# The delta stage's group loop: a value product ahead of the third gate, transposes, copies and activations in another order

## The reference, cut to what matters

```
qkv = silu(causal_conv1d(x @ W_qkvz, conv_weight))         # 4 taps
attn = -(k_beta @ k.T) * decay_mask, strictly lower         # chunks of 64 tokens
attn = row-by-row correction of attn, + I                   # inverse of a triangular matrix
v = attn @ v_beta;  k_cum = attn @ (k_beta * exp(g))
for each chunk:                                             # carries state
    v_prime = v_c - k_cum_c @ state
    out     = (q_c @ state) * exp(g) + intra @ v_prime
    state   = state * exp(g_last) + (k_c * decay).T @ v_prime
out = rmsnorm(out * silu(z), norm_weight) @ W_out
```

## Time and profile before

| | |
|---|---|
| median of three runs | 1714.47 us (1711.51 to 1717.37) |
| the profiled execution's own time | 1714.89 us |
| its span, first to last instruction | 1713.2 us |
| mean granted PE clock over the span | 0.915 of full speed |
| PE / DVE / ACT / POOL busy, share of the span | 83% / 67% / 50% / 46% |
| loop over the groups, about | 550 to 1570 us |
| from one `l1p` on PE to the next | 61.9 to 66.4 us |

### The profile page before, as it was taken

One profiled execution on the slowest core, in us unless ns is written; L12 is line 12 of the kernel. 1 busy time (PEld: TensorE's weight loads), 2 busy tenths in 40 slices (PEclk: granted clock), 3 DMA queues, 4 the chain that ended last, 5 costly groups with the idle time before them and its releaser, 6 DMA issues. The chain is left out here.

```text
span 1713.2 us, 38604 instructions
## 1 busy us (share of the span) xinstructions
PE 1428.9 (83%) x14345; PEld 1025.2 (60%) x14345; DVE 1139.4 (67%) x2334; ACT 856.3 (50%) x2403; POOL 780.6 (46%) x1118
## 2 busy tenths in 40 slices
PE   5888993199555889999999999999999999986665
PEld 2443442166422667767767767767777777775465
DVE  6886127823566778788778777778788878643623
ACT  3334861043043575665665665665665666532122
POOL 5000000277114266456556466556566656553343
PEclk9998996599776999999999999999999999988688
DMA  8100005085813464554555555654555545241783
GB/s 280 66 2 2 2 1 154 7 234 178 254 49 88 107 146 124 147 149 134 139 146 139 128 152 134 139 147 142 133 147 149 137 143 151 76 117 56 223 259 128
DMA packets 249434, 218.72 MB, mean 128 GB/s; under 512 B 88770, under 2 KB 224962, under 8 KB 247200
## 3 DMA queue, kind: packets, MB, share of 16 engines
q1 hardware_dynamic: 234992, 192.41, 41.4%
q0 software_dynamic: 5712, 15.60, 2.8%
q10 hardware_dynamic: 8544, 8.26, 1.5%
HBM read 133.85 MB, written 82.25 MB: 126 GB/s over the span
## 5 line engine op out<-in xcount | busy, mean ns | idle before, releaser
L1544 PE MATMUL d_big<-all_xn_t,all_w 128*128 128x512 f32 x512 | 264.2, 649 | 17.3 <-DVE d_conv L1805 11.4
L1805 DVE SCALAR_TENSOR_TENSOR d_conv<-d_big,all_cw,d_conv 128x1023 f32<-128x1023 f32 (+2 forms) x192 | 245.4, 1278 | 46.4 <-ACT d_conv L2039 43.8
L2277 POOL TENSOR_TENSOR d_y<-d_y,all_xn 128x256 f32<-128x256 f32 x128 | 95.8, 748 | 183.9 <-DVE d_y L1952 153.0
L1544 PEld LDWEIGHTS d_big<-all_xn_t,all_w 128*128 128x128 f32 x512 | 98.2, 207 | 107.8 <-issue 96.7
L2141 ACT COPY d_ys<-d_big 128x128 f32<-128x128 f32 x256 | 60.9, 266 | 198.5 <-PE d_big L1695 139.5
L1733 PE MATMUL d_big<-all_wo,d_yt 128*128 128x256 f32 x512 | 126.5, 393 | 13.6 <-DVE d_yt L1877 13.6
L1666 PE MATMUL d_big<-all_w,all_xn_t 128*128 128x256 f32 x512 | 124.2, 386 | 0.0
L1851 DVE SCALAR_TENSOR_TENSOR d_AI<-d_big,d_b_col,d_decay 128x256 f32<-128x256 f32 x256 | 105.7, 474 | 23.0 <-PE d_big L1557 20.7
L1733 PEld LDWEIGHTS d_big<-all_wo,d_yt 128*128 128x128 f32 x512 | 97.4, 198 | 26.4 <-issue 14.1
L1666 PEld LDWEIGHTS d_big<-all_w,all_xn_t 128*128 128x128 f32 x512 | 93.6, 190 | 18.3 <-issue 7.2
L347 DVE TENSOR_REDUCE a_neg_max<-a_big 128x1 f32<-128x128 f32 (+7 forms) x128 | 90.5, 751 | 13.1 <-PE a_big L276 12.8
(11 more groups left out here) (437 smaller groups left out, 3503.5 us busy)
## 6 DMA issues: line engine op xcount, KB each, us to landing
turned_kq_scratch<-d_turned SPq DMA_DIRECT2D x32, 512.0 KB, 3.9
d_kq_tok<-turned_kq_scratch SPq DMA_DIRECT2D x128, 128.0 KB, 3.1
turned_v_scratch<-d_vs SPq DMA_DIRECT2D x16, 1024.0 KB, 4.1
d_vs<-turned_v_scratch SPq DMA_DIRECT2D x64, 256.0 KB, 5.6
grouped_y_scratch<-d_yx SPq DMA_DIRECT2D x32, 512.0 KB, 3.9
d_yx<-grouped_y_scratch SPq DMA_DIRECT2D x128, 128.0 KB, 3.1
all_w<-in_L_attn_W_qkvz SPq DMA_DIRECT2D x16, 768.0 KB
l_hold<-in_L_ffn_gate_up_proj SPq DMA_DIRECT2D x48, 192.0 KB, 3.4
```

The source lines that it names most:

```text
L1544: mm = pe.matmul(big[0][:, c, :], w_sb[par][:, k, n * DK:(n + 1) * DK], xn_t[:, k, c * 512:(c + 1) * 512], start=(k == 0), stop=(k == KD - 1))
L1805: dve.scalar_tensor_tensor(conv[:, sh:T], src[:, 0:T - sh], cw[:, bass.ds(g, 1), COLUMN_OF[j], 3 - sh], conv[:, sh:T], ALU.mult, ALU.add). ...
L2277: pool.tensor_tensor(part, part, zs[:, t, :], ALU.mult).then_inc(s["yg_s"], 1)
```

## The change

In `PE_ORDER`, `prev iv 7` moves from behind `gates 3` to just ahead of `gates 2`, and `l2y` moves ahead of `products 2`. In `DVE_ORDER`, `gather 7` goes between tap 1 and tap 2 of projection 1, the first two transposes `l0x 0`, `l0x 1` go ahead of its tap 3, DVE's `l1p` goes right behind that tap, followed by the third transpose, and only then `kq_turn 1`; `l2p` goes ahead of `products 0`. In `ACT_ORDER`, `l1p` goes ahead of `silu 1`, `gates 3` directly behind `silu 1`, and all four `ksq` and `decay` behind it. To allow this `l0x` is split into three steps of one transpose each. The computation, the tiles and the semaphore counts are the same.

```diff
-    l0y 2, gates 2, l0y 3, l0y 4, l0y 5, l0y 6, l0y 7, gates 3; prev iv 7; this l1p 0, l1p 1, l1p 2, l1p 3; next proj 2
+    l0y 2; prev iv 7; this gates 2, l0y 3, l0y 4, l0y 5, l0y 6, l0y 7, gates 3, l1p 0, l1p 1, l1p 2, l1p 3; next proj 2
...
-            def l0x(g, par):
-
-                for n, q in enumerate((0, 2, 1)):
-                    own = slice(QB * q, QB * q + QB)
-                    half_of = slice(QB * (q % 2), QB * (q % 2) + QB)
-                    dve.wait_ge(s["y0_s"], g * 4 + n + 1)
-                    dve.transpose(Xc[own, :, half_of], Y[own, :, own]).then_inc(s["x0_s"], 1)
+            def l0x(g, par, n):
+
+                q = (0, 2, 1)[n]
+                own = slice(QB * q, QB * q + QB)
+                half_of = slice(QB * (q % 2), QB * (q % 2) + QB)
+                dve.wait_ge(s["y0_s"], g * 4 + n + 1)
+                dve.transpose(Xc[own, :, half_of], Y[own, :, own]).then_inc(s["x0_s"], 1)
```

More of the change, by code:

```diff
@@ L1209 @@
     0, l0p 1, l0p 2, l0p 3, l0p 4; next proj 1 0; this l0p 5, l0p 6, l0p 7; prev qs 7; next proj 1 1; this l0y 0, l0y 1,
-    l0y 2, gates 2, l0y 3, l0y 4, l0y 5, l0y 6, l0y 7, gates 3; prev iv 7; this l1p 0, l1p 1, l1p 2, l1p 3; next proj 2
-    0, proj 2 1; this l1y 0, l1y 1, l1y 2, l1y 3; next products 0; this l2p 0, l2p 1; next products 1, products 2; this
-    l2y 0, l2y 1; next products 3; this y 0, kv 0, iv 0, ks 1; prev out_mm 0 0; this y 1, qs 1, kv 1, iv 1, ks 2, qs 2;
+    l0y 2; prev iv 7; this gates 2, l0y 3, l0y 4, l0y 5, l0y 6, l0y 7, gates 3, l1p 0, l1p 1, l1p 2, l1p 3; next proj 2
+    0, proj 2 1; this l1y 0, l1y 1, l1y 2, l1y 3; next products 0; this l2p 0, l2p 1; next products 1; this l2y 0, l2y 1;
+    next products 2, products 3; this y 0, kv 0, iv 0, ks 1; prev out_mm 0 0; this y 1, qs 1, kv 1, iv 1, ks 2, qs 2;
     prev out_mm 0 1; this y 2, kv 2, iv 2, ks 3, y 3, qs 3, kv 3, iv 3; next proj 3 0; this ks 4; next proj 3 1; this y
@@ L1218 @@
     prev state 6; this v_turn 0; prev r 7, gather 5; this v_turn 1; next tap 0 1, tap 0 2, tap 0 3; this qe; next
-    kq_turn 0; prev gather 6; this l0p; next shift, tap 1 1, tap 1 2, tap 1 3; prev gather 7; this l0x; next kq_turn 1;
-    this l1p; prev y_turn 0; next kb; this l1y; next products 0; this l2p; next products 1; this l2y; next products 2;
+    kq_turn 0; prev gather 6; this l0p; next shift, tap 1 1; prev gather 7; next tap 1 2; this l0x 0, l0x 1; next tap 1
+    3; this l1p, l0x 2; next kq_turn 1; prev y_turn 0; next kb; this l1y, l2p; next products 0, products 1; this l2y; next products 2;
     this state 0, gather 0, r 1; next products 3; this state 1, gather 1; next tap 2 1; this r 2; next tap 2 2; this
@@ L1228 @@
     prev sq2 0, o1 5, sq2 1, ys 6, sq2 2, sq2 3; this silu 3; next tap0 0; this gates 0; prev ys 7, o1 6; next silu 0;
-    this gates 1; prev sq2 4, o1 7; next tap0 1; prev sq2 5; this gates 2, l0y; next silu 1, ksq 0, ksq 1, ksq 2; this
-    l1p; next ksq 3, decay; this gates 3, l1y, l2p; prev sq2 6, sq2 7; this l2y, ys 0; next tap0 2; this ys 1, o1 1;
+    this gates 1; prev sq2 4, o1 7; next tap0 1; prev sq2 5; this gates 2, l0y, l1p; next silu 1; this gates 3; next ksq 0, ksq 1, ksq 2, ksq 3,
+    decay; this l1y, l2p; prev sq2 6, sq2 7; this l2y, ys 0; next tap0 2; this ys 1, o1 1;
     next qsq 0; this ys 2, o1 2, ys 3, o1 3; next silu 2, qsq 1; this ys 4; next tap0 3; this o1 4, ys 5
```

## The result

The changed kernel took a median of 1749.73 us (1742.34 to 1759.92, four runs), the kernel before in the same session 1714.72 (1711.51 to 1717.37, four runs). The ratio is 1.018, 95% interval 1.0125 to 1.0243: **slower by 1.8%**, where I had forecast 1710 us and a range up to 1732. The profiled execution took 1742.34 us, 32.5 more than the 1709.8 of my sum and 27.4 more than the profiled execution of before. Here and in the experiments medians are of all runs and ratios of the fast ones, which leaves three executions of one later kernel (1710 to 1717 us, at a lower clock than its others) out of the ratios.

A forecast was written before the change was run, and what follows sets the result against it. PE bounds, with a 1.90 us wait ahead of `l1p` and clock falls behind; 0.25 x 14 = 3.5 us plus 1.6 in the last group gave 1714.89 - 5.1 = 1709.8, forecast 1710 us, own range 1700 to 1718, with rivals 1689 to 1732.

The forecast's parts named there:

- my sum: Whole kernel: 5.1 us gained in all, 1714.89 - 5.1 = 1709.8 us for the profiled execution.
- The new wait: PE ahead of `l2p`: idle of about 1.2 us, released by DVE's copy `l1y`, which stands behind `kb`.
- The interval of a clean group: From the old `l1p` place to `y 0` without a clock fall: 13.85 us instead of 13.89.
- A: PE ahead of `l2p`: the new idle seldom pulls the clock down, one group in ten; 1690 us; chance 0.24.
- E: Ahead of `l1p`: ACT's copies, not DVE's list, hold the transposes, so the wait stays; 1713 us; chance 0.04.
- D: ACT in the sweep: the moved table load makes `ys 4` 0.9 us late in 15 groups; 1723 us; chance 0.04.
- the price of a fall: PE from `l2p` to `y 0`: each clock fall costs 3.4 us, against 1.7 in `proj 2`.
- the share: Groups whose clock falls behind the new wait: half again, 0.5, seven of 14.
- the first group: `kb` is held by POOL already there, so this group gains nothing.
- the two long ones of before: Clock falls of some 6.8 us over `l2p` and `l2y`, costing 3.4 us each, taken as model for new falls.
- rival C: DVE's `kb` runs into POOL's `vs`; each hit costs 4.7 us, in five groups 1733 us; chance 0.10.
- B: PE ahead of `l2p`: the new idle pulls the clock down nearly always, share 0.85; 1726 us; chance 0.16.

The follow-up runs named there:

- e1: Changed kernel with products 2 back between l2p and l2y on PE, DVE's products 0 and 1 back ahead of l2p and l2y; 1719.5 us, ratio 1.0024 to before.
- f4: Changed kernel with two products repeated right behind products 1, between l2p and l2y, as a control; 1726.0 us, ratio 1.0035 to before.
- e3: Changed kernel with two product matmuls of the next group repeated in PE's wait ahead of l2p; 1696.8 us, ratio 0.9886 to before.
- f2: e4 with products 1 ahead of l2p on PE, so l2y follows l2p directly; 1706.8 us, ratio 0.9926 to before.
- e4: Changed kernel with ksq 0 (two squares) moved ahead of l1p on ACT; 1693.7 us, ratio 0.9789 to before.
- f3: Kernel before with two products repeated in PE's wait ahead of l1p, filling about half of it; 1727.6 us, ratio 1.0039 to before.
- g3: Kernel before with PE's wait ahead of l1p wholly filled, twice the repeated product matmuls of f3; 1722.7 us, ratio 1.0033 to before.
- f1: e4 with the filling of e3 ahead of l2p added; 1704.3 us, ratio 0.9905 to before.

## Why the prediction was wrong

**Right, point by point.** PE's wait ahead of `l1p`: 0.26 (I said 0.4). The new wait, its place, releaser and size: 1.42 for 1.2. `kb` 1309.83 - 1302.94 = 6.89 behind `l1p` (6.8). `y 0` 15.48 behind `l1p` (15.5). The interval of a clean group: unchanged. From `y 0` to the next `l1p`: 1364.77 - 1318.42 = 46.35, which is within 0.05 the 48.03 of before less the 1.64 by which `l1p` is earlier. No fall over `proj 2`. So A and E are refuted, and D too: ACT's `ys 4` still has idle ahead of it, with the load in front of `silu 2`. Timeline of ACT, to set beside the earlier trace rows:

```profile
1331.35 1.28 ACT L2051 ACT_TABLE_LOAD   x1
1332.64 1.06 ACT L2051 ACTIVATE d_vt<-d_conv 128x1024 f32<-128x1024 f32 x1
...
1335.74 0.45 ACT L2141 COPY d_ys<-d_big 128x128 f32<-128x128 f32 x2 [0.45 <-ACT d_junk L2070]
```

The load takes 1.28 us and `silu 2` starts 0.01 behind it. The Trainium skill ("ScalarE: Activation LUTs", What ACT_TABLE_LOAD costs) adds a drain of 1380 ns to it; the trace shows none here, nor in front of the load: the activation ahead of it ends at 1331.33.

**The step that failed is the price of a fall**, with the share beside it: 0.5 x 3.4 us a group, 23.8 in 14. Nine groups fell, not seven; at 3.4 us each they would have cost 30.6. They cost 50.2. So 6.8 of what was missing is the share and 19.6 the price, the longer waits of two groups with it. By groups of the changed kernel, above 21.45 us each:

| | groups | us |
|---|---|---|
| wait of 1.4, then a fall of 10.2 us | 5 | 21.4, that is 4.3 each |
| `kb` held up by `vs`, wait of 3.0 to 3.2, a fall of 13.7 | 2 | 15.3 |
| PE stops 1.7 or 2.4 us in `l1y`, a fall of 13.7 | 2 | 13.5 |
| no fall | 5 | 0.4 |

That is 50.6 where I had 23.8. With the first group (5.6 worse, where I had said no gain and no loss: its wait ahead of `l2p` is 4.46 and it falls for 13.7 instead of 3.4) and the last (1.1 gained, not 1.6) it is 26.8 + 5.6 + 0.5 = 32.9, against the 32.5 by which the profiled execution missed my sum.

Three errors are in it. I took the length of a fall from the two long ones of before (6.8 us), in which products 1 and 2 still stood between `l2p` and `l2y`, although the same change moves `products 2` away: e1 and f4 show that what stands there decides between 3.4 to 6.8 and 10 to 14 us. That makes 4.3 us for a plain fall where I had 3.4. Second, my rival C, which I gave one chance in ten, did happen, not in five groups but in two and in the first one; I priced it at 4.7 and it cost 7.7, because the longer wait drew a longer fall. DVE of such a group, and POOL at that time:

```profile
905.39 1.89 DVE L1831 TENSOR_TENSOR d_kxb<-l_cols,d_b_col 128x16 f32<-128x16 f32 x1
```

```profile
905.34 1.91 POOL L2234 TENSOR_TENSOR d_vs<-d_vs,d_sv 128x1024 f32<-128x1024 f32 x1 [6.97 <-DMA d_vs<-turned_v_scratch]
```

The instruction takes 0.18 us elsewhere. In the clean group `kb` ended 0.33 us ahead of `vs`, where I had reckoned 0.75; over the other groups the distance runs from 1.7 us to none. A few tenths of a us decide whether they meet. Third, I saw that the two long falls of before came behind stops in `l1y` and priced them with the rest; in the changed kernel two groups of that kind cost 6.7 each (in before 4.5 and 6.1), 2.9 more in all. They are no part of the share of groups that the wait decides.

And rivals A and B were set up as one question, how often the clock falls. The count did not change, nine of 14 in both kernels. What changed was the length.

What stays open: why the clock falls behind one wait of 1.41 and not behind another (five of eight groups with it), and how many groups fall, and for how long, in an execution other than the profiled one.

## What to carry to other kernels

Price a wait by what stands beside it. With one product ahead of it and small matmuls, a product and small matmuls behind it, 1.4 us of idle cost 4.0 to 4.7 us more through the clock in five of eight groups, and with the falls gone (e3) the same order was faster than before. Full matmuls behind a wait made the falls shorter (e1, f4); that they help ahead of it too is my guess from f2 against e4. Two matmuls whose result nobody reads were worth their microsecond in e3, and not in the kernel before (f3, g3) nor on top of the shorter wait (f1): measure such a filling, don't assume it. When a wait moves, look at the lengths of the falls it will meet in the new place, not only at their number. And the source of a wait is worth more than its place: one pair of squares moved ahead on ACT gave 1.5 to 2.1% over the kernel before (1.3 and 1.6% by the medians of all executions), where the change without it lost 1.8%.

## What the runs showed of the hardware

PE stops in the middle of `l1y`, 96 matmuls of 32x32 that take 1.2 us when nothing stops them, for 0.4 to 3.2 us, released by nothing in the profile ("issue"). The traces hold the fetches of instructions as DMA packets on queue q8, 16 KiB each, one in some 11 us. In g3 such a fetch begins 2.4 to 2.8 us before the end of each of the nine stops in `l1y`, and 2.4 to 3.0 before the end of each of the five in the kernel before. Not every fetch beside `l1y` stops PE: in the first group of before one begins 0.1 us into it, and it still takes 1.2. DMA queues in the stretch 628 to 631, with the stop that ends at 630.62 (queue, packets, MB, share of the DMA engines):

```profile
q1 hardware_dynamic: 405, 0.41, 43.1%
q8 instruction: 1, 0.02, 2.3%
```

Up to this stop the DMA engines were busy with the kernel's own transfers; the stretch 620 to 630 us has a DMA share of 0.89:

```profile
620.00:630.00 10.00, 8.36 (x147) 5.44 (x146) 6.62 (x12) 9.63 (x24) 3.83 (x4) 1.00 0.89 221
```

The Trainium skill ("Runtime: NRT & Kernel Launch", Instruction fetch mechanics) says that the sequencer fetches its own instructions in blocks of 16 KiB, 256 instructions, and that this is mostly hidden; the 0.02 MB of the row agree with the size. I read the stops as fetches that are not hidden, because small matmuls use up a block faster than it comes. By that reading, adding instructions anywhere in a group moves the block limits against `l1y`, for better or worse: f3 and g3 add 8 and 16 a group (with their weight loads), and the stops in `l1y` went from 6.2 us in 600 to 1477 to 13.3 and 13.7; e3, f1 and f4 add the same 8 and have 5.3, 4.6 and 3.2, where the changed kernel has 5.3. That the fetch causes the stops is read from the traces; no run took it away.
